# A graph network kernel whose per-graph tail is done for two graphs at a time

## The chip, the cores and the metric

The kernel runs on one core of a Trainium2 chip. The metric is device time in microseconds. TensorE does the matmuls, VectorE and ScalarE the elementwise work out of PSUM, GpSimd elementwise work between SBUF tiles, and SyncE's queue most of the transfers.

## What is computed

There are B = 128 graphs of N = 128 nodes with F = 64 features, the hidden width is H = 192 and the output width 64.

```python
# layer 0, per graph
h   = relu(layernorm(x))
P   = h @ (W1a + W1b) + b1 ;  Q = h @ W1b
hm[j]  = sum over neighbours k of relu(P[j] - Q[k])     # mask = adj > 0
x   = x + hm @ W2 + deg * b2
# layer 1, per graph
h   = relu(layernorm(x))
x   = x + (adj @ h) @ W3.T
```

Each node has some 12% of the others as neighbours. So the kernel doesn't form all 128 x 128 pairs: it numbers the neighbours of each node, and a one-hot matrix per neighbour number picks the row of Q.

## The kernel before

The mask of a graph is turned into codes (a running count of the neighbours) in a set-up that takes about the first 60 us. Then come 128 steps, one per graph, and 4 more to drain the pipeline (`TAIL`). Each engine has its own hand-written `step(b, u)`; `u` is `b` modulo 12.

**The sums of graph b** go through a ring of three PSUM places of two banks each. Four regular chunks (i = 0 to 3) hold four neighbour numbers each:

- ScalarE copies P into the place (`seed`, L530), which is 768 values per partition.
- TensorE adds the picked rows of -Q with 8 matmuls (`gather`, L378), 4 for each bank.
- VectorE takes relu and adds to the accumulator `acc`, one instruction per bank (`consume`, L763).

A chunk's place can be seeded again only when it has been consumed; ScalarE's seed of chunk 1 of a graph waits for the last `consume` of the graph before. A fifth chunk of three slots holds what is left over for nodes with more neighbours: L406 and L378 fill it, ScalarE's L562 takes its relu into `relu_row`, GpSimd's L864 adds the three slots in two instructions, and `ownerT` sends the sums to their nodes in TensorE's L465.

Between its consumes VectorE writes one-hot matrices for later graphs (L749, one between the two consumes of each chunk), `from_first` (L795, after chunk 0), `owner` (L798, chunk 1), `onehot_row` (L804, three instructions after chunk 2) and the low half of PQ (L680, before chunk 3).

**What follows the sums** is done in the steps after, once per graph:

- Step b+1: TensorE transposes the accumulator (L464, four transposes: two slots, and the 192 columns as 128 and 64 padded to 128) and adds the left-over rows (L465, two matmuls). GpSimd puts deg * b2 onto x (L897, L900).
- Step b+2: ScalarE copies the transposed sums (L556), TensorE multiplies by W2 (L441 and L442, 64 columns wide), VectorE adds to x (L813) and takes statistics (L819).
- Step b+3: VectorE's L790 makes mean and variance, GpSimd's four instructions L873, L874, L880 (the power -0.5) and L883 the scale and shift, ScalarE's L583 the normed h2, TensorE the product with the adjacency (L470).
- Step b+4: L556 copies that too, TensorE multiplies by W3 (L445), VectorE adds to x (L816). SyncE's queue stores every four graphs.

GpSimd's order in a step is: L864 twice, the four instructions of the norm, `start_sums` (L851), the low half of P (L890), the bias (L897, L900), and the halves of h1 (L906, L908). ScalarE's order in a step is: seed of chunk 0, copies L550 and L556, seed of chunk 1, L562, copies L567 and L570, seeds of chunks 2 and 3, PQ and P (L575, L576), then L583, which waits for GpSimd's L883, and L591.

Of the kernel before, what the change touches and what calls it, by code (L numbers as in the profile page):

```python
# [53 lines left out]
def gnn_kernel(nc, x, adjT, W1a, W1b, b1, W2, b2, W3T, CONSTS, out):  # L54
# [15 lines left out]
    with ExitStack() as ctx:  # L70
# [13 lines left out]
        w_parts = sb("w_parts", [N, 2, 3 * H], F16)    # L84

        w2a = sb("w2a", [N, O])
        w2b = sb("w2b", [N, O])
        w3t = sb("w3t", [N, O])
# [53 lines left out]
        ownerT = sb("ownerT", [N, 2, N])  # L142
        code_row = sb("code_row", [N, N], F16)
        start = sb("start", [N, PER_BANK, H])
        acc_space = sb("acc", [N, 2, ROW + N - H2])
        acc = acc_space[:, :, 0:ROW].rearrange("p g (s h) -> p g s h", h=H)
        relu_row = sb("relu_row", [N, ROW_SLOTS, H])

        sums_T = sb("sums_T", [N, 3, N])
        hmT, aggT = sums_T[:, 0:2, :], sums_T[:, 2, :]  # L150
        bias = sb("bias", [N, F])
        stats2 = sb("stats2", [N, 6])
        mv = sb("mv", [N, 2, 2])
        ve2 = sb("ve2", [N, 1])
        neg2 = sb("neg2", [N, 2])
        rstd2 = sb("rstd2", [N, 2])
        shift2 = sb("shift2", [N, 2])
        h2 = sb("h2", [N, 2, F])
# [11 lines left out]
        pq_ps, out1_ps, out2_ps = prep[:, 0:2 * H], prep[:, 2 * H:2 * H + O], prep[:, 2 * H + O:2 * H + 2 * O]  # L170
        sums_T_ps = post[:, 0:3 * N].rearrange("p (k n) -> p k n", k=3)
        h1T_ps = post[:, 3 * N:4 * N]
# [58 lines left out]
        sums_T_ready = sem("sums_T_ready")  # L231
# [13 lines left out]
        HEAD, TAIL = 3, 4  # L245
# [42 lines left out]
        def mixed_at(b, u, t):  # L288

            return (u - 3) % BODY, (b - 3) // BODY if isinstance(b, int) else t - 1 if u < 3 else t  # L290
# [21 lines left out]
        def _(sp):  # L312
# [15 lines left out]
            for b in range(3, B + TAIL):  # L328
                if BODY <= b - 3 + BODY < B:
                    sp.wait_ge(transposed, b + 3)  # L330
                    adj(b - 3 + BODY)
                done = b - TAIL + 1
                if done > 0 and done % STORE == 0:
                    sp.wait_ge(y_ready, done)
                    sp.dma_start(out[:, done - STORE:done, :], x_all[:, done - STORE:done, :]).then_inc(stored, 16)
            sp.wait_ge(stored, 16 * B // STORE)

        @block.tensor
        def _(pe):
# [42 lines left out]
            def step(b, u, looped=False, t=None):  # L382
                main = exists(b)
                parts = PQ[:, u % 2]
                for i in range(CHUNKS):
# [25 lines left out]
                    if i == 0 and main:  # L411
# [3 lines left out]
                        if exists(b - 2):  # L415
                            pe.wait_ge(sums_T_ready, b - 1)
                        else:
                            pe.wait_ge(h1T_ready, b + 2)
# [537 lines left out]
```

## Time and profile before

| | |
|---|---|
| time, median of 3 runs | 905.98 us (905.89 to 906.07) |
| time of the profiled execution | 904.65 us |
| its span, first to last instruction | 902.6 us |
| busy share of the span | TensorE 96%, VectorE 96%, ScalarE 86%, GpSimd 77% |
| mean granted TensorE clock | 0.983 of full speed |

The span is what the trace covers, and the execution's time has 2 us around it. Busy spans of neighbouring instructions of one engine overlap in the records, so an engine shown as almost always busy may still have waited; the starts have to be compared.

### The profile page before, as it was taken

To read this page: it belongs to the slowest core of one execution; us is meant where nothing else is said; L and a number is where in the kernel's file an instruction comes from. 1 tells how busy PE (TensorE), PEld (TensorE's weight loads), DVE (VectorE), ACT (ScalarE), POOL (GpSimd) and SP (SyncE) were. 2 spreads that over 40 slices of the span, in tenths; PEclk is the share of its full clock that TensorE was granted. 3 is DMA by queue.
4 is the path that set the end of the run, shared out by engine and by line. 5 is a ranking of instruction groups with operands and counts; after the bars stand their busy time and mean duration, and the time that the engine had idled before them with its cause. 6 is when DMAs were issued, how large, how long until landed. Compare 5 with 4: busy or idle time off the path is not lost.

```text
span 902.6 us, 27715 instructions
## 1 busy us (share of the span) xinstructions
PE 862.0 (96%) x8626; PEld 771.7 (86%) x8627; DVE 866.4 (96%) x3032; ACT 775.9 (86%) x1728; POOL 698.8 (77%) x1548
## 2 busy tenths in 40 slices
PE   3879999999999999999999999999999999999996
PEld 1448999989998989999999999998999899989995
DVE  6989999999999999999999999999999999999993
ACT  4858989898989898989889898988898889898983
POOL 0857787888888888888887878787878788888874
PEclk9789999999999999999999999999999999999997
DMA  9700000000000000000000000000000000000000
GB/s 341 279 1 5 20 11 20 16 20 17 19 17 20 11 20 17 20 17 20 15 14 16 20 17 19 17 18 18 12 20 16 20 16 20 16 20 11 7 8 16
DMA packets 26549, 27.58 MB, mean 31 GB/s; under 512 B 3360, under 2 KB 24352, under 8 KB 25376
## 3 DMA queue, kind: packets, MB, share of 16 engines
q1 hardware_dynamic: 25488, 25.37, 8.3%
q8 instruction: 72, 1.18, 0.6%
q14 instruction: 77, 0.63, 0.2%
q10 hardware_dynamic: 912, 0.39, 0.2%
HBM read 21.56 MB, written 4.19 MB: 29 GB/s over the span
## 4 chain that ended last, share of the span: by engine, by line
PE 69%; DVE 19%; issue 5%; ACT 3%; POOL 2%; DMA 1%; SPq 0%; ACTq 0%; POOLq 0%; DVEq 0%
PE ring L378 36%; DVE acc L763 12%; PE ring L406 6%; PE post L465 4%; PE post L464 4%; PE prep L435 4%; PE post L470 4%; PE prep L445 3%; PE prep L442 2%; DVE onehot_space L749 2%; PE prep L441 2%; ACT ring L530 1%; POOL rstd L915 1%; DMA x_all<-x_nbf_dram 1%; DVE onehot_row L804 1%
## 5 line engine op out<-in xcount | busy, mean ns | idle before, releaser
L763 DVE SCALAR_TENSOR_TENSOR acc<-ring,acc 128x384 f32<-128x384 f32 x896 | 489.0, 546 | 1.1 <-PE ring L378 0.2
L530 ACT COPY ring<-P 128x768 f32<-128x768 f32 x512 | 403.3, 811 | 16.3 <-DVE acc L763 6.9
L378 PE MATMUL ring<-PQ,onehot_space 128*128 128x192 f16 x4096 | 404.0, 247 | 7.2 <-ACT ring L530 3.3
L378 PEld LDWEIGHTS ring<-PQ,onehot_space 128*128 128x128 f16 x4096 | 338.2, 100 | 31.7 <-ACT ring L530 19.2
L864 POOL TENSOR_TENSOR relu_row<-relu_row 128x192 f32<-128x192 f32 x256 | 151.8, 593 | 101.1 <-ACT relu_row L562 91.1
L749 DVE TENSOR_SCALAR onehot_space<-mask_all 128x512 f16<-128x512 f16 x512 | 155.2, 305 | 0.0
L583 ACT ACTIVATE h<-x_all,shift,rstd 128x64 f32<-128x64 f32 x128 | 56.3, 440 | 83.6 <-POOL shift L883 83.6
L851 POOL TENSOR_SCALAR start<-P,spare 128x192 f32<-128x192 f32 x128 | 121.1, 946 | 5.9 <-ACT P L576 5.1
L464 PE MATMUL post<-consts,acc 128*128 128x128 f32 x512 | 98.5, 274 | 1.5 <-POOL relu_row L864 1.5
L465 PE MATMUL post<-ownerT,relu_row 128*128 128x128 f32 x512 | 99.0, 275 | 0.0
L406 PE MATMUL ring<-PQ,owner 128*128 128x384 f16 (+1 forms) x512 | 94.1, 306 | 0.0
L880 POOL TENSOR_TENSOR rstd<-ve,half_power 128x1 f32<-128x1 f32 x128 | 89.4, 698 | 0.0
L378 PE MATMUL ring<-PQ,onehot_row 128*128 128x192 f16 x768 | 84.3, 246 | 0.4 <-DVE onehot_row L804 0.4
L562 ACT ACTIVATE relu_row<-ring 128x576 f32<-128x576 f32 x128 | 82.5, 644 | 0.6 <-PE ring L378 0.6
L763 DVE SCALAR_TENSOR_TENSOR acc<-ring,start 128x384 f32<-128x384 f32 x128 | 71.3, 557 | 11.4 <-PE ring L378 1.6
L465 PEld LDWEIGHTS post<-ownerT,relu_row 128*128 128x128 f32 x512 | 77.3, 191 | 0.0
L378 PEld LDWEIGHTS ring<-PQ,onehot_row 128*128 128x128 f16 x768 | 65.2, 98 | 9.2 <-DVE onehot_row L804 1.1
L890 POOL TENSOR_TENSOR PQ<-P,PQ 128x192 f16<-128x192 f32 x128 | 70.5, 551 | 2.7 <-ACT P L576 2.7
L406 PEld LDWEIGHTS ring<-PQ,owner 128*128 128x128 f16 x512 | 50.5, 99 | 18.2 <-issue 0.2
L575 ACT CAST PQ<-prep 128x384 f16<-128x384 f32 x128 | 63.9, 499 | 0.7 <-PE prep L437 0.7
L470 PE MATMUL post<-adj_again,h 128*128 128x128 f32 x256 | 62.0, 324 | 2.1 <-ACT h L583 2.1
L435 PE MATMUL prep<-w_parts,h1T 128*128 128x384 f16 x256 | 62.9, 328 | 0.9 <-ACT h1T L550 0.9
(129 smaller groups left out, 1616.0 us busy)
## 6 DMA issues: line engine op xcount, KB each, us to landing
onehot_space<-adj_kbj_dram SPq DMA_DIRECT2D x8, 1024.0 KB, 17.1
adj_again<-adj_kbj_dram SPq DMA_DIRECT2D x128, 64.0 KB, 1.9
x_all<-x_nbf_dram SPq DMA_DIRECT2D x8, 512.0 KB, 17.8
out_dram<-x_all SPq DMA_DIRECT2D x32, 128.0 KB, 1.7
consts<-consts_dram SPq DMA_DIRECT2D x1, 192.0 KB, 2.6
scratch<-w1a_dram ACTq DMA_DIRECT2D x2, 48.0 KB, 4.3
scratch<-w1b_dram ACTq DMA_DIRECT2D x2, 48.0 KB, 6.7
scratch<-b_dram ACTq DMA_DIRECT2D x1, 96.0 KB, 10.0
```

The source lines that it names most:

```text
L378: last = nc.tensor.matmul(to, hot(s), parts[:, part, H:2 * H], start=False, stop=(part == 1), skip_group_check=True)
L406: nc.tensor.matmul(slots[place(u, i)][:, bank_, 0:n, :], owner[:, u % 2, :], parts[:, part, 0:H].unsqueeze(1).broadcast_to([N, n, H]), sta ...
L435: nc.tensor.matmul(pq_ps, h1T[:, :], w_parts[:, part, 0:2 * H], start=(part == 0), stop=False, skip_group_check=True)
L464: nc.tensor.matmul(sums_T_ps[:, k, :], hm, ident, start=(s == 0), stop=False, is_transpose=True)
L465: last = nc.tensor.matmul(sums_T_ps[:, k, :], hm_row[:, k * N:(k + 1) * N], ownerT[:, (u + 1) % 2, :], start=False, stop=True)
L470: last = nc.tensor.matmul(sums_T_ps[:, 2, :], h2[:, :, :], adj_again[:, at, :], start=True, stop=True)
L530: return nc.scalar.copy(slots[to], src.unsqueeze(1).unsqueeze(1).broadcast_to([N, BANKS, PER_BANK, H]))
L749: return nc.vector.tensor_scalar(onehot[:, hot_of(u), i, s, :, :], code_kj[:, bass.ds(b, QUAD), :], 2.0 * (SLOTS * i + s) + 1.0, None, ALU ...
L763: return nc.vector.scalar_tensor_tensor(sums, slots[to][:, bank_], 0.0, start[:, :, :] if first else sums, ALU.max, ALU.subtract if first ...
L851: nc.gpsimd.tensor_scalar(start[:, 0, :], P[:, u % 2, :], spare[:, b:b + 1], 0.0, ALU.mult, ALU.max).then_inc(start_ready, 1)
L864: last = nc.gpsimd.tensor_tensor(sums, sums, relu_row[:, s, :], ALU.add)
L880: nc.gpsimd.tensor_tensor(rstd2[:, k:k + 1], ve2[:, :], half_power[:, :], ALU.pow).then_inc(rstd2_ready, 1)
```

## The change

Graphs are taken in pairs of an even and an odd one. The diff cut to its core (the set-up of the new tiles, the helper functions that count semaphores and the names of tiles are left out; `pairs`, `transposes` and `mixes` only give the counts to wait for):

```diff
-        HEAD, TAIL = 3, 4
+        HEAD, TAIL = 3, 5
...
 # TensorE, i == 1
+                            order = slice((u + 1) % 2 * N, (u + 1) % 2 * N + H)
...
-                        if exists(b - 2):
-                            nc.tensor.matmul(out1_ps, hmT[:, 0, :], w2a[:, :], start=True, stop=False)
-                            last = nc.tensor.matmul(out1_ps, hmT[:, 1, :], w2b[:, :], start=False, stop=True)
-                        if exists(b - 4):
-                            last = nc.tensor.matmul(out2_ps, aggT[:, :], w3t[:, :], start=True, stop=True)
+                        if u % 2 and exists(b - 3):
+                            nc.tensor.matmul(out_ps, tailT, w2b[:, :, :], start=True, stop=False, skip_group_check=True)
+                            for g in range(2):
+                                last = nc.tensor.matmul(out_ps[:, g, :], hmT[g], w2a[:, :], start=False, stop=True, skip_group_check=True)
+                        if u % 2 == 0 and exists(b - 6):
+                            last = nc.tensor.matmul(out_ps, aggT, w3t[:, :, :], start=True, stop=True)
 # TensorE, i == 3: the head (128 columns) of each graph, the tails (64 + 64) of a pair at once
+                            for s in range(PER_BANK):
+                                nc.tensor.matmul(head_ps, acc_space[:, (u - 1) // 2 % 2, s, heads[(u - 1) % 2]], ident, start=(s == 0), stop=False, is_transpose=True)
+                            last = nc.tensor.matmul(head_ps, row_heads[(u - 1) % 2], ownerT[:, (u - 1) % QUAD, :], start=False, stop=True)
+                        if u % 2 == 0 and exists(b - 2):
+                            for s in range(PER_BANK):
+                                nc.tensor.matmul(tail_ps, acc_space[:, k // 2, s, tails], ident, start=(s == 0), stop=False, is_transpose=True)
+                            for g in range(2):
+                                last = nc.tensor.matmul(tail_ps, row_tails[g], ownerT[:, k + g, :], start=False, stop=(g == 1))
+                        if u % 2 and exists(b - 5):
+                            for g in range(2):
+                                last = nc.tensor.matmul(agg_ps, h2_padded[g], adj_again[:, at + g, :], start=(g == 0), stop=(g == 1))
 # ScalarE
+                    if i == 0 and u % 2 == 0: nc.scalar.copy(sums_T[:, parts, :], sums_T_ps[:, parts, :])       # 256 wide
+                    if i == 0 and u % 2: nc.scalar.copy(sums_T[:, 2:4, :], sums_T_ps[:, 0:3:2, :])              # 256 wide
                     if i == 1 and exists(b - 1):
                         nc.scalar.activation(relu_rows[(u - 1) % 2], row_slots[place(u, -1)], ACT.Relu)
+                    if i == 1 and u % 2 and exists(b - 5):
+                        norm2(b, u, t, 1)
                     if i == 1 and main:
                         nc.scalar.copy(code_row[:, :], code_row_ps)
...
-                    if i == 4 and exists(b - 3):
+                    if i == 4 and u % 2 == 0 and exists(b - 4):
+                        wait_apart(act, norm2_ready, pairs(b, u, t, -4))
+                        norm2(b, u, t, 0)
 # VectorE
+                    if i == 0 and u % 2 == 0 and exists(b - 4):
+                        for g in range(2):
+                            last = nc.vector.bn_aggr(mv[:, (u - 4) // 2 % 2, g, :], stats2[:, g, :])
+                    if i == 3 and u % 2 and exists(b - 3):
+                        nc.vector.tensor_tensor(x_all[:, pair, :], x_all[:, pair, :], out_ps, ALU.add).then_inc(x1_ready, 1)
+                    if i == 4 and u % 2 and exists(b - 3):
+                        wait_apart(dve, x1_ready, pairs(b, u, t, -3))
+                        for g in range(2):
+                            last = nc.vector.bn_stats(stats2[:, g, :], x_all[:, b - 3 + g, :])
+                    if i == 4 and u % 2 == 0 and exists(b - 6):
+                        nc.vector.tensor_tensor(x_all[:, pair, :], x_all[:, pair, :], out_ps, ALU.add).then_inc(y_ready, 1)
 # GpSimd: the same four instructions of the norm, [N, 2] wide, in even steps alone; the bias [N, 2, F] wide, likewise
+                if u % 2 == 0 and exists(b - 4):
+                    nc.gpsimd.tensor_tensor(rstd2[:, k, :], ve2[:, :], half_power[:, :].broadcast_to([N, 2]), ALU.pow)
```

W2's tail and W3 stand twice in a block-diagonal 128 x 128 matrix; for that two more small loads are issued on ScalarE's queue at the start. The first-layer weights get 128 more columns (a copy on VectorE in the set-up), so that odd graphs come out with their last 64 columns first. `acc` has four buffers in place of two, `relu_row` two in place of one and `ownerT` four in place of two. SyncE's queue loads two adjacency matrices in every second step, and stores when a pair is ready.

## Rows read from the trace of the kernel before

**Rows 1.** VectorE's timeline of one step (start us, us, engine line ...; gaps left out).

```profile
511.47 0.54 DVE L763 SCALAR_TENSOR_TENSOR acc<-ring,acc 128x384 f32<-128x384 f32 x1
...
512.44 0.56 DVE L763 SCALAR_TENSOR_TENSOR acc<-ring,start 128x384 f32<-128x384 f32 x1
...
513.68 0.48 DVE L795 TENSOR_SCALAR from_first<-count_h,first_row 128x128 f16<-128x128 f16 x1
514.07 0.54 DVE L763 SCALAR_TENSOR_TENSOR acc<-ring,acc 128x384 f32<-128x384 f32 x1
514.54 0.39 DVE L749 TENSOR_SCALAR onehot_space<-mask_all 128x512 f16<-128x512 f16 x1
514.85 0.55 DVE L763 SCALAR_TENSOR_TENSOR acc<-ring,acc 128x384 f32<-128x384 f32 x1
...
515.57 0.54 DVE L763 SCALAR_TENSOR_TENSOR acc<-ring,acc 128x384 f32<-128x384 f32 x1
...
516.71 0.38 DVE L804 TENSOR_SCALAR onehot_row<-code_row 128x128 f16<-128x128 f16 x3
...
517.94 0.55 DVE L763 SCALAR_TENSOR_TENSOR acc<-ring,acc 128x384 f32<-128x384 f32 x1
```

**Rows 2.** ScalarE's timeline of the same step.

```profile
512.05 0.80 ACT L530 COPY ring<-P 128x768 f32<-128x768 f32 x1
...
513.64 1.56 ACT L530 COPY ring<-P 128x768 f32<-128x768 f32 x2
...
516.45 0.44 ACT L583 ACTIVATE h<-x_all,shift,rstd 128x64 f32<-128x64 f32 x1 [0.63 <-POOL shift L883]
516.80 0.42 ACT L591 ACTIVATE h<-x_all,shift,rstd 128x64 f32<-128x64 f32 x1
```

**Rows 3.** GpSimd's timeline of the same step, and one power from a step before.

```profile
508.85 0.57 POOL L880 TENSOR_TENSOR rstd<-ve,half_power 128x1 f32<-128x1 f32 x1
...
513.51 1.27 POOL L864 TENSOR_TENSOR relu_row<-relu_row 128x192 f32<-128x192 f32 x2 [0.66 <-ACT relu_row L562]
...
515.35 0.73 POOL L880 TENSOR_TENSOR rstd<-ve,half_power 128x1 f32<-128x1 f32 x1
...
516.39 0.95 POOL L851 TENSOR_SCALAR start<-P,spare 128x192 f32<-128x192 f32 x1
517.31 0.55 POOL L890 TENSOR_TENSOR PQ<-P,PQ 128x192 f16<-128x192 f32 x1
```

**Rows 4.** TensorE's timeline: the gather of chunk 0 consumed at 512.44.

```profile
511.81 0.82 PE L378 MATMUL ring<-PQ,onehot_space 128*128 128x192 f16 x8
```

**Rows 5.** VectorE's timeline of a later step, 615.6 to 622.4.

```profile
615.06 0.54 DVE L763 SCALAR_TENSOR_TENSOR acc<-ring,acc 128x384 f32<-128x384 f32 x1
...
616.08 0.56 DVE L763 SCALAR_TENSOR_TENSOR acc<-ring,start 128x384 f32<-128x384 f32 x1
...
617.66 0.55 DVE L763 SCALAR_TENSOR_TENSOR acc<-ring,acc 128x384 f32<-128x384 f32 x1
...
620.29 0.53 DVE L804 TENSOR_SCALAR onehot_row<-code_row 128x128 f16<-128x128 f16 x3
...
621.89 0.55 DVE L763 SCALAR_TENSOR_TENSOR acc<-ring,acc 128x384 f32<-128x384 f32 x1
```

**Rows 6.** GpSimd's timeline of that later step.

```profile
620.26 1.04 POOL L851 TENSOR_SCALAR start<-P,spare 128x192 f32<-128x192 f32 x1
...
621.27 0.55 POOL L890 TENSOR_TENSOR PQ<-P,PQ 128x192 f16<-128x192 f32 x1
```

**Rows 7.** Groups by line and shape (busy us, mean ns of one record | idle before).

```profile
L442 PE MATMUL prep<-w2b,sums_T 128*128 128x64 f32 x256 | 49.7, 276 | 0.0
...
L816 DVE TENSOR_TENSOR x_all<-x_all,prep 128x64 f32<-128x64 f32 x128 | 26.6, 208 | 3.7 <-PE prep L445 3.7
```

**Rows 8.** Timeline of the set-up: a 32-wide power on GpSimd.

```profile
51.48 5.44 POOL L915 TENSOR_TENSOR rstd<-mom,half_power 128x32 f32<-128x32 f32 x1
```

**Rows 9.** The same stretch on VectorE.

```profile
53.77 2.72 DVE L749 TENSOR_SCALAR onehot_space<-mask_all 128x512 f16<-128x512 f16 x13
```

More of the change, by code:

```diff
@@ L286, in hot_of, with agg_at, transposes, mixes @@
             return u // QUAD % HOT_QUADS
-        def mixed_at(b, u, t):
-            return (u - 3) % BODY, (b - 3) // BODY if isinstance(b, int) else t - 1 if u < 3 else t
+        def agg_at(b, u, t):
+            return (u - 5) % BODY, (b - 5) // BODY if isinstance(b, int) else t - 1 if u < 5 else t
+        def transposes(step):
+            return step + 2 if isinstance(step, int) and step > B + 1 else step + 3
+        def mixes(step):
+            return step + 1 if isinstance(step, int) and step > B + 2 else step + 2
+        def pairs(b, u, t, d):
+            return (b + d) // 2 + 1 if isinstance(b, int) else t * (BODY // 2) + (u + d) // 2 + 1
         def load(eng, which, b):
@@ L326, in _ @@
                 adj(b)
[L328 to L332, printed above, removed]
+            for b in range(0, B, 2):
+                done = b - 2
                 if done > 0 and done % STORE == 0:
-                    sp.wait_ge(y_ready, done)
+                    sp.wait_ge(y_ready, done // 2)
                     sp.dma_start(out[:, done - STORE:done, :], x_all[:, done - STORE:done, :]).then_inc(stored, 16)
+                if b + BODY < B:
+                    sp.wait_ge(transposed, transposes(b + 5))
+                    adj(b + BODY)
+                    adj(b + BODY + 1)
+            sp.wait_ge(y_ready, B // 2)
+            sp.dma_start(out[:, B - STORE:B, :], x_all[:, B - STORE:B, :]).then_inc(stored, 16)
             sp.wait_ge(stored, 16 * B // STORE)
@@ L432, in step @@
+                        last = None
                         if exists(b + 1):
                             pe.wait_ge(h1T_ready, b + 2)
+                            order = slice((u + 1) % 2 * N, (u + 1) % 2 * N + H)
                             for part in range(2):
-                                nc.tensor.matmul(pq_ps, h1T[:, :], w_parts[:, part, 0:2 * H], start=(part == 0), stop=False,
+                                nc.tensor.matmul(pq_ps, h1T[:, :], w_parts[:, part, 0:2, order], start=(part == 0), stop=False,
@@ L466, in step @@
[L466 to L471 removed]
+                            if not main:
+                                pe.wait_ge(even_T_ready, pairs(b, u, t, -2))
```

225 lines of the change are left out of this document (115 added, 110 removed).

## The prediction

> **What bounds the kernel now.** The busy line (in the table ahead) has TensorE and VectorE both at 96%, which doesn't say which of them sets the pace. So I took one step of the timeline and asked of each start what it had waited for. All offsets count from T, the end of a graph's last consume: 511.47 + 0.54 = 512.01 [rows 1]. The next such end is 517.94 + 0.55 = 518.49, 6.48 later; the consumes at 512.44 and at 616.08 lie 16 steps apart [rows 1, 5], 103.64 / 16 = 6.48 us on average. 128 steps make 829 of the 902.6 us.
>
> In this step chunk 0 is consumed at +0.43, chunk 1 at +2.06 and +2.84, chunk 2 at +3.56, and it ends at +6.48 [rows 1]. In the later step T is 615.60; chunk 0 comes at +0.48, but chunk 1 at +2.06 again [rows 5]. So what holds chunk 1 isn't chunk 0. It is GpSimd: L864 starts at +1.50 and its two instructions end at +2.77 [rows 3], the first, by halves, near +2.10. VectorE's L795 lies across that end (513.68, 0.48 long, with the next start 0.39 behind it) and L749 across the end of the second (0.39 long, the next start 0.31 behind); chunk 1's second consume starts 0.07 after GpSimd's end [rows 1, 3]. L749 takes 2.72 / 13 = 0.21 from start to start when it isn't held [rows 9]. I read this as VectorE's f16 instructions and GpSimd's two-input instructions excluding each other. GpSimd's start in turn hangs on T: ScalarE seeds chunk 1 at +0.04 [rows 2], then takes the relu that L864 waits for. This circle (T, seed, relu, L864, chunk 1, 4.42 of VectorE's own work, next T) is 6.48 long and closes by itself. VectorE also waits for chunk 0's gather, 511.81 to 512.44 [rows 4, 1], but has caught up by chunk 1.
>
> **The change, part by part.** *TensorE.* Per pair two transposes, one L442 and one L445 go; the remaining ones of the last two are twice as wide. L442 has 49.7 / 128 = 0.39 us of busy time per graph [rows 7], overlaps included. Four instructions less in a pair, none longer than that, are at most 0.8 us per pair, and half of it if half of the busy time is overlap: I take 0.2 to 0.4 us per graph. It is worth nothing where GpSimd sets chunk 1; without that cover it would be worth the wait for chunk 0, which is the first rival.
>
> *VectorE.* Two of four adds per pair go (L816: 208 ns each [rows 7]) and two become wider; in return `bn_stats` now stands right behind the add on which it waits. Between 0 and 0.2 us per pair, ahead of chunk 0, under the same cover: nothing in even steps.
>
> *GpSimd, even steps.* Chunk 1 is as before. Then the norm's four instructions come for two graphs. The power of 32 values takes 5.44, that of one 0.73 [rows 8, 3], so a second value costs (5.44 - 0.73) / 31 = 0.15; the other three I take as unchanged, being two values wide. So L851 moves from 516.39 (+4.38) to +4.53 and L890 behind it from an end at 517.86 (+5.85) to +6.00 [rows 3]. VectorE's L804 runs at 516.71 (+4.70) [rows 1], now 0.17 behind L851's start in place of 0.32. The later step shows what comes of that: there L851 started at 620.26, +4.66 or 0.28 late, L804 took 0.53 for 0.38, and the last consume started 0.07 after L890's end, at 621.89, +6.29 in place of +5.93 [rows 5, 6, 1]: 0.36 lost for 0.28 of lateness. With L890's end at +6.00 the last consume starts at +6.07, 0.14 late. The bounds are 0 (the second value hides) and 0.36. I take **+0.15 in even steps**, 6.63.
>
> *GpSimd, odd steps.* The norm falls away (L880 to L851 is 1.04 [rows 3]), and the six instructions of norm and bias come once in two steps. GpSimd isn't on the path there; nothing counted.
>
> *VectorE, odd steps.* Ahead of chunk 0 stands one add alone, and no `bn_aggr`, so L795 can start near +1.3, before L864, and isn't held. Chunk 2 could then come at about +2.95, 0.6 early.
>
> *ScalarE, odd steps.* But a second L583 (`norm2(..., 1)`) now stands between the relu of chunk 4 and the two copies and seeds of chunks 2 and 3. It occupies 516.80 - 516.45 = 0.35 [rows 2]. Chunk 2's seed moves from 513.64 (+1.63) to +1.98 and ends 0.80 later, at +2.78 [rows 2]; a gather start to its first consume takes 512.44 - 511.81 = 0.63 [rows 4, 1], with 0.05 for the signal (an estimate from 512.01 to 512.05 for the seed). That is +3.46, against +3.56 before. So **-0.10 in odd steps**: VectorE waits for ScalarE instead. The bounds are -0.6 (the seed isn't late) and +0.1.
>
> *ScalarE, rest.* L556 copies 256 columns in place of 384, 0.1 a step; it idled 0.63 a step [rows 2], and idles on. In even steps L583 comes 0.15 later with GpSimd, and the next seed of chunk 1 with it, but T is 0.15 later as well.
>
> *Queues, set-up, tail.* SyncE's transfers keep their number, in twos; nothing waits for them with 12 buffers. The two new small loads and VectorE's one weight copy lie in the set-up, beside adjacency loads: 0 to 1 us. The drain has one step more, but its transposes no longer stand before the same step's product with the adjacency: -1 to +1. I count 0 for both.
>
> *Sum.* 62 pairs in steady state x (+0.15 - 0.10) = +3.1 us. The profiled execution took 904.65 (span 902.6), so it would come to 907.8; the median of the runs stands 1.3 above it, at 905.98, and goes to **909.1**, which I write 909.0. Own range of this case: both edits uncertain by 0.1 per pair, 902 to 915. A measurement tells some 0.2% (1.8 us) here.
>
> At one place the Trainium skill speaks against the change more strongly than the rows do. Its page "SBUF — State Buffer", section "Who interferes with whom", says that VectorE and GpSimd share one pair of ports as an exclusive lock, held for the whole instruction, so that the second to come blocks fully. The first half is what L864 shows. The second half disagrees with rows 8 and 9: thirteen L749 ran 0.21 apart while the 5.44 us power was in flight. By that rule a longer L880 would also hold chunk 2's L749; it is the third rival.
>
> **The rivals.** *1. TensorE's relief counts* (0.20). If VectorE's wait for chunk 0 is what really sets the step, and L864 only follows, each step loses it: chunk 0 came 0.43 after T, and VectorE's own work in between is two adds and one statistics (208 ns each at most [rows 7], overlapping), so 0.11 to 0.15 goes. 128 x 0.11 to 0.15 = 14 to 19 us: 887 to 892, written 890. For it speaks TensorE's 96%; against it chunk 1 at +2.06 whether chunk 0 was at +0.43 or +0.48 [rows 1, 5].
>
> *2. The second power hides* (0.22). L880 took 0.57 in one step and 0.73 in the next [rows 3], and the spread is as large as a second value's price. If the short form becomes the rule, L851 isn't late, even steps stay at 6.48 or gain a little, and the pair is 0.10 shorter: 62 x -0.10 = -6, so 900. Against it: 0.57 may just be the form that VectorE didn't disturb, and the order of the two engines at that point doesn't change.
>
> *3. The lateness feeds itself* (0.20). Place: L880 to L890 in even steps. If the longer L880 (+3.34 to +4.22) runs into L749 of chunk 2, at 3.56 + 0.47 = +4.03, each delays the other, by 0.06 on VectorE (4.22 + 0.07 against 4.03 + 0.20) and more on GpSimd. It decides from the point where L851 is 0.28 late, as at 620.26; then an even step costs 0.36 [rows 5, 6]. 62 x (0.36 - 0.10) = +16: 922 at the worst, 918 with half of the excess. The case with the lock held for the whole instruction ends here too.
>
> **How the numbers follow.** Forecast 0.38, rival 1 0.20, rival 2 0.22, rival 3 0.20. Faster by over 0.2% (below 904.2): rival 1 whole, 0.20, most of rival 2, 0.16 (if small gains fall short it is within), and of the forecast's own range its lowest tenth, 0.02: 0.38. Within 0.2%: the rest of rival 2, 0.06, and 0.12 of the forecast: 0.18. Slower: 0.24 of the forecast and rival 3: 0.44. The range leaves out the better half of rival 1 and the worst tail of rival 3: 891 to 918.
>
> **What would show it.** Even and odd steps of different lengths, near 6.63 and 6.38. In even steps chunk 1 at +2.06, L880 near 0.88, L851 near +4.53, a longer L804 group, and the last consume 0.07 after L890. In odd steps L795 not held, chunk 1 near +1.5 and an idle VectorE ahead of chunk 2, released by TensorE behind ScalarE's L530. TensorE with more idle time and no gain from it. Wrong would be: chunk 1 of even steps ahead of L864's end (rival 1), L851 at +4.4 (rival 2), or an odd step whose chunk 2 isn't held.

## The result and the profile after

The changed kernel took 913.1 us (911.7 to 914.0, 4 runs), against 906.03 before; the ratio is 1.0077, with a 95% interval of 1.0057 to 1.0097. So it is slower by 0.8%. (Before: three runs from 905.89 to 906.07 and a fourth of 2185 us, which moves the median by 0.05 and is not in the ratio.)

The page of the changed kernel: its span, busy times, and two groups (busy us, mean ns of one | idle before, releaser).

```profile
span 909.7 us, 26109 instructions
...
PE 842.6 (93%) x8242; PEld 718.0 (79%) x8243; DVE 851.5 (94%) x2908; ACT 761.9 (84%) x1728; POOL 614.1 (68%) x1164
...
L808 DVE SCALAR_TENSOR_TENSOR acc<-ring,acc 128x384 f32<-128x384 f32 x896 | 490.3, 547 | 27.7 <-PE ring L400 26.8
...
L904 POOL TENSOR_SCALAR start<-P,spare 128x192 f32<-128x192 f32 x128 | 120.0, 938 | 96.5 <-ACT P L618 95.7
```

Every engine does less work, TensorE by 19.4 us, VectorE by 14.9, GpSimd by some 85, and the kernel is longer. (L808 is the consume, before L763; L904 the start of the sums, before L851; L943 the low half of P, which completes PQ and is called the halves of PQ below, before L890; L918 the row sums, before L864; L960 and L962 the split of h into halves, before L906 and L908; L794 the one-hot, before L749; L851 is now VectorE's one-hot rows, before L804; L933 the power, before L880.)

To split the 7.1 us of span, one line per kernel is enough: a step's first consume, with its first and last start. Before:

```profile
L763 DVE SCALAR_TENSOR_TENSOR acc<-ring,start x128: 532/558/560, 58.9 to 881.7; 128x384 f32<-128x384 f32 x128
```

and after:

```profile
L808 DVE SCALAR_TENSOR_TENSOR acc<-ring,start x128: 539/558/559, 60.3 to 889.2; 128x384 f32<-128x384 f32 x128
```

The set-up is 1.4 longer, the 127 steps between are 828.9 in place of 822.8, so 6.1 longer (6.527 each in place of 6.479), and what follows is 0.4 shorter. Now one even and one odd step, with offsets from T, the end of a graph's last consume. VectorE's timeline of the changed kernel:

```profile
516.32 0.55 DVE L808 SCALAR_TENSOR_TENSOR acc<-ring,acc 128x384 f32<-128x384 f32 x1
...
518.93 0.54 DVE L808 SCALAR_TENSOR_TENSOR acc<-ring,acc 128x384 f32<-128x384 f32 x1
...
520.89 0.28 DVE L794 TENSOR_SCALAR onehot_space<-mask_all 128x512 f16<-128x512 f16 x1
521.09 0.54 DVE L808 SCALAR_TENSOR_TENSOR acc<-ring,acc 128x384 f32<-128x384 f32 x1
521.56 0.54 DVE L851 TENSOR_SCALAR onehot_row<-code_row 128x128 f16<-128x128 f16 x3
...
522.75 0.39 DVE L794 TENSOR_SCALAR onehot_space<-mask_all 128x512 f16<-128x512 f16 x1
523.06 0.54 DVE L808 SCALAR_TENSOR_TENSOR acc<-ring,acc 128x384 f32<-128x384 f32 x1
...
525.12 0.55 DVE L808 SCALAR_TENSOR_TENSOR acc<-ring,acc 128x384 f32<-128x384 f32 x1
...
527.04 0.56 DVE L808 SCALAR_TENSOR_TENSOR acc<-ring,acc 128x384 f32<-128x384 f32 x1 [0.44 <-PE ring L400]
...
529.41 0.55 DVE L808 SCALAR_TENSOR_TENSOR acc<-ring,acc 128x384 f32<-128x384 f32 x1
```

and GpSimd's in the even one of the two:

```profile
520.01 0.23 POOL L929 TENSOR_SCALAR neg<-mv 128x2 f32<-128x2 f32 x1
520.21 1.00 POOL L933 TENSOR_TENSOR rstd<-ve,half_power 128x2 f32<-128x2 f32 x1
521.35 0.20 POOL L936 TENSOR_TENSOR shift<-neg,rstd 128x2 f32<-128x2 f32 x1
521.53 0.94 POOL L904 TENSOR_SCALAR start<-P,spare 128x192 f32<-128x192 f32 x1
522.44 0.55 POOL L943 TENSOR_TENSOR PQ<-P,PQ 128x192 f16<-128x192 f32 x1
```

T is 516.32 + 0.55 = 516.87, 523.60 and 529.96. The even step is 6.73 long, the odd one 6.36. In the even step chunk 1 comes at 518.93, +2.06 as before. The power lasts 1.00, the start of the sums comes at +4.66 in place of +4.38 [rows 3], the one-hot rows take 0.54 for 0.38 [rows 1], the last L794 0.39 for 0.28 (before: the line below), and the last consume starts 0.07 behind L943's end, 522.99. The two lengthened instructions are 0.16 + 0.11 = 0.27, and 6.73 - 0.27 is 6.46.

```profile
517.74 0.28 DVE L749 TENSOR_SCALAR onehot_space<-mask_all 128x512 f16<-128x512 f16 x1
```

In the odd step chunk 1 comes at +1.52, then VectorE waits 0.44 for the gather of chunk 2, which comes at +3.44. Such pairs are 0.13 longer than two steps of before (2 x 6.479); 64 of them would be 8.3, and 6.1 were measured, so not all pairs are of this form. In the middle of the run (steps 10 to 115, 53 pairs) the pairs are 6.1 longer together, 0.115 each: four of the even steps there take 6.47 to 6.61, and two of the steps before take 6.73 and 6.84. The steps in which the pipeline fills and drains differ little.

### The profile page after: what moved, and what is told of

The parts are those of the page before. It is cut to its first block, busy times and chain, and to the rows that moved or that the text cites. A ratio compares the mean times of both kernels' runs of the same rounds, so it can differ in the third digit from the quotient of the medians.

```text
span 909.7 us, 26109 instructions
## 1 busy us (share of the span) xinstructions
PE 842.6 (93%) x8242; PEld 718.0 (79%) x8243; DVE 851.5 (94%) x2908; ACT 761.9 (84%) x1728; POOL 614.1 (68%) x1164
## 4 chain that ended last, share of the span: by engine, by line
DVE 52%; PE 19%; issue 16%; ACT 9%; DMA 1%; POOL 1%; SPq 0%; DVEq 0%; ACTq 0%; POOLq 0%
DVE acc L808 31%; PE ring L400 10%; DVE onehot_space L794 7%; ACT ring L561 5%; DVE onehot_row L851 4%; DVE PQ L725 3%; PE prep L465 2%; PE prep L457 2%; DVE stats L865 2%; ACT row_space L604 1%; DVE x_all L861 1%; DMA x_all<-x_nbf_dram 1%; PE prep L463 1%; DVE mv L836 1%; DVE owner L845 1%
## 5 line engine op out<-in xcount | busy, mean ns | idle before, releaser
L808 DVE SCALAR_TENSOR_TENSOR acc<-ring,acc 128x384 f32<-128x384 f32 x896 | 490.3, 547 | 27.7 <-PE ring L400 26.8
L400 PE MATMUL ring<-PQ,onehot_space 128*128 128x192 f16 x4096 | 412.5, 247 | 32.5 <-ACT ring L561 19.9
L400 PEld LDWEIGHTS ring<-PQ,onehot_space 128*128 128x128 f16 x4096 | 319.6, 98 | 97.4 <-ACT ring L561 50.0
L918 POOL TENSOR_TENSOR row_space<-row_space 128x192 f32<-128x192 f32 x256 | 151.8, 593 | 125.7 <-ACT row_space L604 115.6
L904 POOL TENSOR_SCALAR start<-P,spare 128x192 f32<-128x192 f32 x128 | 120.0, 938 | 96.5 <-ACT P L618 95.7
L794 DVE TENSOR_SCALAR onehot_space<-mask_all 128x512 f16<-128x512 f16 x512 | 155.1, 305 | 0.0
L566 ACT ACTIVATE h<-x_all,shift,rstd 128x64 f32<-128x64 f32 x128 | 55.5, 434 | 60.0 <-POOL shift L936 60.0
L604 ACT ACTIVATE row_space<-ring 128x576 f32<-128x576 f32 x128 | 82.4, 644 | 0.7 <-PE ring L400 0.7
L808 DVE SCALAR_TENSOR_TENSOR acc<-ring,start 128x384 f32<-128x384 f32 x128 | 71.3, 557 | 5.2 <-PE ring L400 2.6
L943 POOL TENSOR_TENSOR PQ<-P,PQ 128x192 f16<-128x192 f32 x128 | 70.0, 547 | 2.7 <-ACT P L618 2.7
L933 POOL TENSOR_TENSOR rstd<-ve,half_power 128x2 f32<-128x2 f32 x64 | 62.1, 971 | 0.0
L851 DVE TENSOR_SCALAR onehot_row<-code_row 128x128 f16<-128x128 f16 x384 | 59.2, 208 | 0.0
L631 ACT ACTIVATE h<-x_all,shift,rstd 128x64 f32<-128x64 f32 x128 | 57.5, 449 | 0.1
L960 POOL TENSOR_SCALAR h_parts<-h 128x64 f16<-128x64 f32 x128 | 54.4, 425 | 2.9 <-ACT h L631 2.9
L487 PE MATMUL post<-consts,acc 128*128 128x128 f32 x256 | 49.7, 276 | 1.8 <-issue 1.8
```

What stands on the lines that cost most here:

```text
L400: last = nc.tensor.matmul(to, hot(s), parts[:, part, H:2 * H], start=False, stop=(part == 1), skip_group_check=True)
L604: nc.scalar.activation(relu_rows[(u - 1) % 2], row_slots[place(u, -1)], ACT.Relu).then_inc(relu_row_ready, 1)
L794: return nc.vector.tensor_scalar(onehot[:, hot_of(u), i, s, :, :], code_kj[:, bass.ds(b, QUAD), :], 2.0 * (SLOTS * i + s) + 1.0, None, ALU ...
L808: return nc.vector.scalar_tensor_tensor(sums, slots[to][:, bank_], 0.0, start[:, :, :] if first else sums, ALU.max, ALU.subtract if first ...
L851: last = nc.vector.tensor_scalar(onehot_row[:, s, :], code_row[:, :], 2.0 * (COVERED + s) + 1.0, None, ALU.is_equal)
L904: nc.gpsimd.tensor_scalar(start[:, 0, :], P[:, u % 2, :], spare[:, b:b + 1], 0.0, ALU.mult, ALU.max).then_inc(start_ready, 1)
```

## The experiments

Twelve kernels ran. "Start" below is the start of the sums on GpSimd; offsets are again from T. The diffs are cut to the lines that matter; waits and semaphore increments that only follow from the new order, and `.then_inc(...)` at the ends of lines, are left out.

**e1, the power alone.** GpSimd's power is taken for the even graph of a pair only; the odd graph's is left out (its `rstd` is 1). All else is the changed kernel.

```diff
-nc.gpsimd.tensor_tensor(rstd2[:, k, :], ve2[:, :], half_power[:, :].broadcast_to([N, 2]), ALU.pow)
+nc.gpsimd.tensor_tensor(rstd2[:, k, 0:1], ve2[:, 0:1], half_power[:, :], ALU.pow)
```

> The changed kernel with GpSimd's power for the even graph of a pair alone (the scale of odd graphs stays at 1.0: the power of the second graph is left out). Everything else stays paired. Theory (GpSimd's lateness in even steps): the power falls from 0.97 to 0.70 us, L851 starts 0.27 earlier, even steps fall from 6.73 to 6.47, odd steps stay at 6.36. 62 pairs x 0.26 = 16 us: 897 us, ratio to the kernel before 0.990. Rival (the lost time lies in the paired TensorE and VectorE work or in the set-up, GpSimd has room at 68% busy): 911 to 913, ratio 1.006 to 1.008.

Measured: 902.4 us, ratio to the kernel before 0.9973 (0.9962 to 0.9984). The power's group in e1 and in the changed kernel (ns min/median/max):

```profile
L934 POOL TENSOR_TENSOR rstd<-ve,half_power x64: 557/722/724, 88.6 to 893.1; 128x1 f32<-128x1 f32 x64
```

```profile
L933 POOL TENSOR_TENSOR rstd<-ve,half_power x64: 715/1001/1006, 88.7 to 902.2; 128x2 f32<-128x2 f32 x64
```

The whole loss hangs on this one instruction, which is 0.28 us shorter 64 times: the even steps fall from 6.73 to 6.47. The odd steps came out longer than expected, 6.47 for 6.36, so that less was gained than 16 us: with T 0.26 earlier, GpSimd's split of h (L963 here) now lies across VectorE's first L795 of the next step, which lasts 0.44, and `from_first` is caught by the row sums:

```profile
518.63 0.56 DVE L809 SCALAR_TENSOR_TENSOR acc<-ring,start 128x384 f32<-128x384 f32 x1
519.11 0.44 DVE L795 TENSOR_SCALAR onehot_space<-mask_all 128x512 f16<-128x512 f16 x1
519.47 0.55 DVE L809 SCALAR_TENSOR_TENSOR acc<-ring,acc 128x384 f32<-128x384 f32 x1
519.93 0.54 DVE L843 TENSOR_SCALAR from_first<-count_h,first_row 128x128 f16<-128x128 f16 x1
520.39 0.54 DVE L809 SCALAR_TENSOR_TENSOR acc<-ring,acc 128x384 f32<-128x384 f32 x1
```

With T at 518.34 chunk 1 is at +2.05 again, in an odd step, whose early chunk 1 is lost. GpSimd's start comes at +4.23 there, and the one-hot rows, 0.45 behind it, are not lengthened (GpSimd first, then VectorE):

```profile
522.57 1.03 POOL L905 TENSOR_SCALAR start<-P,spare 128x192 f32<-128x192 f32 x1 [1.48 <-ACT P L618]
```

```profile
523.02 0.38 DVE L852 TENSOR_SCALAR onehot_row<-code_row 128x128 f16<-128x128 f16 x3
```

**e2, the odd graph's norm on ScalarE** moved from ahead of chunk 2's seed to behind chunk 3's.

```diff
-                    if i == 1 and u % 2 and exists(b - 5):
+                    if i == 3 and u % 2 and exists(b - 5):
                         norm2(b, u, t, 1)
```

> The changed kernel with ScalarE's norm of the odd graph moved from behind the relu of chunk 4 to behind the seed of chunk 3, so that the seeds of chunks 2 and 3 come 0.35 us earlier in odd steps. Theory (ScalarE's queue holds chunk 2 in odd steps): chunk 2's seed goes from +1.95 to +1.62, its first consume from +3.44 to about +3.1 at the latest, and odd steps from 6.36 to about 6.0, unless VectorE's own work is what is left; even steps stay at 6.73. 62 x 0.3 = 19 us: 894, range 890 to 900. Rival (VectorE or TensorE is the bound in odd steps, and the seed only looks late): 911 to 914.

Measured: 909.0 us, ratio 1.0042 (1.0026 to 1.0059). Chunk 2 came 0.23 earlier, and 0.16 of it went to the next collision. VectorE's rows in an odd step of e2 (T = 522.24; GpSimd's start is at 526.47, +4.23):

```profile
525.45 0.56 DVE L808 SCALAR_TENSOR_TENSOR acc<-ring,acc 128x384 f32<-128x384 f32 x1 [0.22 <-PE ring L400]
...
526.59 0.55 DVE L851 TENSOR_SCALAR onehot_row<-code_row 128x128 f16<-128x128 f16 x3
```

The rows take 0.55 there, and 0.39 in the changed kernel, where GpSimd's start is at +4.23 too but the rows come 0.23 later.

**e3, the norm split:** the odd graph's power and shift go into the odd step, behind the row sums, and its ScalarE norm to the step's end.

```diff
+                if u % 2 and exists(b - 5):
+                    nc.gpsimd.tensor_tensor(rstd2[:, k, 1:2], ve2[:, 1:2], half_power[:, :], ALU.pow)
+                    nc.gpsimd.tensor_tensor(shift2[:, k, 1:2], neg2[:, k, 1:2], rstd2[:, k, 1:2], ALU.mult)
```

> The changed kernel with GpSimd's power and shift split: the even graph's in the even step, the odd graph's in the odd step behind L864, and ScalarE's norm of the odd graph at the end of the odd step, as in the even step. TensorE, VectorE, bias, variance and mean stay paired. Theory: both holds go at once: even steps 6.47, odd steps near 6.0; pair 12.5 against 13.1: 62 x 0.6 = 37 us: 876, range 870 to 885, and below the kernel before, since the wait on TensorE and two instructions of VectorE are really saved. Rival (the holds are the old ones and the paired work isn't worth anything): 905 to 907, as before the change.

Measured: 931.8 us, ratio 1.0284 (1.0261 to 1.0308), the largest miss so far. VectorE and GpSimd in an odd step of e3 (T = 519.27):

```profile
524.14 0.89 DVE L854 TENSOR_SCALAR onehot_row<-code_row 128x128 f16<-128x128 f16 x3
```

```profile
523.19 0.93 POOL L907 TENSOR_SCALAR start<-P,spare 128x192 f32<-128x192 f32 x1 [0.23 <-ACT P L618]
524.09 0.55 POOL L953 TENSOR_TENSOR PQ<-P,PQ 128x192 f16<-128x192 f32 x1
```

GpSimd isn't late here, it is early: its start came at +3.92, and the halves of PQ lie right across the one-hot rows, 0.89 for 0.38. So "GpSimd late" can't be the whole rule.

**e4, TensorE's relief alone**, in the kernel before: the transposes and the product of the last 64 columns of the accumulator are left out.

```diff
-                            nc.tensor.matmul(out1_ps, hmT[:, 0, :], w2a[:, :], start=True, stop=False)
-                            last = nc.tensor.matmul(out1_ps, hmT[:, 1, :], w2b[:, :], start=False, stop=True)
+                            last = nc.tensor.matmul(out1_ps, hmT[:, 0, :], w2a[:, :], start=True, stop=True)
...
-                                for s in range(PER_BANK):
+                                for s in range(PER_BANK if k == 0 else 0):
```

> The kernel before the change, with TensorE's two transposes of the last 64 columns and the multiplication by W2's tail left out (the last 64 columns of the sums of regular chunks don't reach the output): some 0.44 us less TensorE work per graph, more than the 0.33 that the change saves. Theory (chunk 1 is held by GpSimd's L864): steps stay at 6.47 to 6.48, 904 to 906, ratio 0.998 to 1.0. Rival 1 of the prediction (VectorE's wait for chunk 0's gather sets the step): 887 to 892, ratio 0.98.

Measured: 903.6 us, ratio 0.9985 (0.9976 to 0.9995). The line of its first consumes:

```profile
L762 DVE SCALAR_TENSOR_TENSOR acc<-ring,start x128: 535/558/560, 59.7 to 881.1; 128x384 f32<-128x384 f32 x128
```

A step is 6.468 for 6.479: TensorE's spare time is worth 0.01 a step, not the 0.11 to 0.15 of the first rival. How much was taken off is less than expected, though: TensorE's busy time falls from 862.0 to 846.6 us, 0.12 a graph and not 0.44, while the change took off 0.15 a graph. So e4 tests nearly the relief of the change, not more than it.

**e5, the wide power in the kernel before**, every step, its second value unused.

```diff
-nc.gpsimd.tensor_tensor(rstd2[:, k:k + 1], ve2[:, :], half_power[:, :], ALU.pow)
+nc.gpsimd.tensor_tensor(rstd2[:, k, :], ve2[:, :], half_power[:, :].broadcast_to([N, 2]), ALU.pow)
```

> The kernel before the change, with GpSimd's power (L880) computed on two columns in every step, the second a copy that nobody reads: the suspected cost of the change alone, twice as often. Theory (a GpSimd that is 0.27 us late at L851 and L890 holds VectorE's L804 and the one-hot matrix of chunk 3): every step goes from 6.47 to 6.73, 128 x 0.26 = 33 us: 938, ratio 1.036. Rival (GpSimd is busy 77% of the span and the wait is taken up, only TensorE's L470 gets later and VectorE catches up behind L864): 906 to 909.

Measured: 933.4 us, ratio 1.0314 (1.0282 to 1.0347). The power's group is 1.00 as in the changed kernel, and the first consume runs from 58.8 to 908.6, 6.69 a step:

```profile
L880 POOL TENSOR_TENSOR rstd<-ve,half_power x128: 724/1002/1005, 81.3 to 921.8; 128x2 f32<-128x2 f32 x128
```

So the second value alone costs about 0.21 in each step that has it, in a kernel that has nothing else of the change. (The `ve` ahead of the power is two values wide as well there, and lasts 0.22 at either width.)

**e6, power first.** In the changed kernel the power stands right behind `ve`, the variance with epsilon; the start of the sums and PQ follow, negation and shift come behind them, and ScalarE's norms move to the odd step.

```diff
-                    nc.gpsimd.tensor_scalar(neg2[:, k, :], mv[:, k, :, 0], -1.0, None, ALU.mult)
...
-                    nc.gpsimd.tensor_tensor(shift2[:, k, :], neg2[:, k, :], rstd2[:, k, :], ALU.mult)
...
                         start_sums(b + 1, u + 1)
...
+                    nc.gpsimd.tensor_scalar(neg2[:, k, :], mv[:, k, :, 0], -1.0, None, ALU.mult)
...
+                    nc.gpsimd.tensor_tensor(shift2[:, k, :], neg2[:, k, :], rstd2[:, k, :], ALU.mult)
```

> The changed kernel with GpSimd's order turned: the pair's power right behind the epsilon, then L851 and L890, and the negated mean and the shift behind them; ScalarE norms both graphs in the odd step (one behind the relu of chunk 4, one at the end). All work is there and paired, the 0.97 us power too. Theory: L851 starts at +4.2 to +4.4 in even steps, 0.3 earlier than in the changed kernel, and they fall to 6.47; odd steps stay at 6.36 if the one-hot matrix of chunk 0 gets the port before GpSimd's L962 (else 6.47, as most of them in the run with the narrow power). 897 to 903, ratio 0.992 to 0.998. Rival (the two-wide power costs its 0.27 us wherever it stands): 911 to 914.

Measured: 929.9 us, ratio 1.0278 (1.0261 to 1.0295), far off. VectorE and GpSimd in an even step of e6 (T = 513.50):

```profile
517.51 0.45 DVE L791 TENSOR_SCALAR onehot_space<-mask_all 128x512 f16<-128x512 f16 x1
...
518.35 0.76 DVE L848 TENSOR_SCALAR onehot_row<-code_row 128x128 f16<-128x128 f16 x3
```

```profile
516.64 0.72 POOL L929 TENSOR_TENSOR rstd<-ve,half_power 128x2 f32<-128x2 f32 x1
517.40 0.94 POOL L901 TENSOR_SCALAR start<-P,spare 128x192 f32<-128x192 f32 x1
518.31 0.55 POOL L936 TENSOR_TENSOR PQ<-P,PQ 128x192 f16<-128x192 f32 x1
```

Two things are new. The two-value power takes 0.72, not 1.00, when it is over before the one-hot of chunk 2 begins. And GpSimd is early again: start at +3.90, both one-hot groups longer, the even step 7.02.

**e7, e3 with one more wait:** in odd steps GpSimd's start waits until the one-hot rows are written.

```diff
+                        if u % 2:
+                            pool.wait_ge(onehot_row_ready, b + 1)
                         start_sums(b + 1, u + 1)
```

> The kernel with the split norm (it took 931.8), with one more wait: in odd steps GpSimd starts L851 only when VectorE has written onehot_row. Theory (there GpSimd was too early, not too busy: L851 at +3.91 and L890 at +4.81 lay on VectorE's one-hot matrix of chunk 2 and on L804, and odd steps took 7.11): the wait takes that away, odd steps fall to 6.47 or below (6.1 to 6.2 where chunk 0 isn't held): 903, range 888 to 906. Rival (four more instructions per pair on GpSimd, or a later start of the sums, are what costs): 925 or above.

Measured: 897.9 us, ratio 0.9921 (0.9904 to 0.9937). An added wait took 34 us out. (The profiled execution took 901.8, the others 897.6 to 898.0, so the trace, with steps of 6.46 and 6.47, doesn't show why e7 ends 7 us under the kernel before.) Start at +5.27 in an odd step of e7 (T = 518.05), behind the rows (0.38):

```profile
522.74 0.38 DVE L854 TENSOR_SCALAR onehot_row<-code_row 128x128 f16<-128x128 f16 x3
```

```profile
523.32 0.93 POOL L907 TENSOR_SCALAR start<-P,spare 128x192 f32<-128x192 f32 x1 [1.59 <-DVE onehot_row L854]
```

**e8, e6 with bias and norms in the odd step,** where GpSimd has its gap.

```diff
+                if u % 2 and exists(b - 3):
+                    nc.gpsimd.tensor_tensor(bias[:, :, :], ...)
+                    nc.gpsimd.tensor_tensor(x_all[:, of, :], x_all[:, of, :], bias[:, :, :], ALU.add)
                     start_sums(b + 1, u + 1)
...
-                if u % 2 == 0 and exists(b - 2):
-                    nc.gpsimd.tensor_tensor(bias[:, :, :], ...)
-                    nc.gpsimd.tensor_tensor(x_all[:, of, :], x_all[:, of, :], bias[:, :, :], ALU.add)
```

> The turned order of GpSimd (power first), and besides the pair's bias (two instructions) moved from the end of even steps into the gap of odd steps between L864 and L851, and both of ScalarE's norms at the end of odd steps, so that chunk 2's seed is early. All work is there. Theory: even steps 6.47; in odd steps chunk 0's one-hot matrix is free, chunk 2 comes at +3.21 and L851 near +3.85, L890 between L804 and the one-hot matrix of chunk 3, so 3.21 + 2.91 = 6.12. Pair 12.6: 62 x -0.36 = -22 against the kernel before: 883, range 878 to 892, ratio 0.975. Rival (the holds only move on to another pair of instructions): 897 or above.

Measured: 920.1 us, ratio 1.0166 (1.0149 to 1.0183). An even step of e8 went from 522.09 to 529.11 and the odd one behind it to 535.29 (ends of last consumes). So the odd half held, 6.18; the even one was 7.02 by e6's collision, which this expectation, made together with e6's, shared.

**e9, one instruction moved:** in the changed kernel the negation goes behind the power, so the power starts 0.2 earlier.

```diff
-                    nc.gpsimd.tensor_scalar(neg2[:, k, :], mv[:, k, :, 0], -1.0, None, ALU.mult)
                     nc.gpsimd.tensor_tensor(rstd2[:, k, :], ve2[:, :], half_power[:, :].broadcast_to([N, 2]), ALU.pow)
+                    nc.gpsimd.tensor_scalar(neg2[:, k, :], mv[:, k, :, 0], -1.0, None, ALU.mult)
```

> The changed kernel with one GpSimd instruction moved: in even steps the negation of the mean stands behind the power instead of ahead of it, so that the power starts 0.2 us earlier. Theory (a power that VectorE's one-hot of chunk 2 doesn't lie across costs 0.72 us for two values, as in the earlier run with the power first; 0.97 is the one-hot in its way, from 4.02 to 4.30 behind T): the power 0.73 in place of 0.97, the start of the sums at +4.38 in place of +4.65, even steps 6.47 in place of 6.73. Odd steps lose some of their gain, as with the narrow power, because the split of h now ends 0.25 later against the new T and lies across VectorE's first one-hot: 6.45. In all 902 us, range 897 to 905. Rival (the second value itself costs 0.25): nothing moves, since the instructions are the same and their sum too: 911 to 913.

Measured: 912.7 us, ratio 1.0085 (1.0071 to 1.0098), as the rival had it, but not for its reason. GpSimd and VectorE in an even step of e9 (T = 516.77):

```profile
519.91 0.73 POOL L932 TENSOR_TENSOR rstd<-ve,half_power 128x2 f32<-128x2 f32 x1
520.72 0.38 POOL L933 TENSOR_SCALAR neg<-mv 128x2 f32<-128x2 f32 x1
521.19 0.20 POOL L936 TENSOR_TENSOR shift<-neg,rstd 128x2 f32<-128x2 f32 x1
521.37 0.99 POOL L904 TENSOR_SCALAR start<-P,spare 128x192 f32<-128x192 f32 x1
```

```profile
520.79 0.28 DVE L794 TENSOR_SCALAR onehot_space<-mask_all 128x512 f16<-128x512 f16 x1
```

The power shrank to 0.73, as the theory had it. But now the negation lies across VectorE's L794 (+4.02 to +4.30), takes 0.38 for 0.23 and ends 0.03 after it, at +4.33. In the changed kernel it was the power that ended at +4.34. VectorE's one-hot holds whichever of these two GpSimd instructions meets it, and lets GpSimd's chain go on at about +4.3 in both.

**e10, e8 with negation and shift ahead of the start again.**

> The kernel with bias and both norms' activations in the odd step (920 us), with one change: negation and shift stand ahead of the start of the sums again, right behind the early power. Theory (that run was slow because in even steps the start of the sums at +3.90 and the halves of PQ at +4.81 came too early and lay across the one-hot of chunk 2 and the one-hot rows): start at +4.38, the halves at +5.28 behind the one-hot rows, even steps 6.47 in place of 7.02; odd steps stay at 6.18. 62 x (0.55) less: 886 us, range 880 to 894; it would beat both kernels and every run so far. Rival (something else in that order is slow, a wait of ScalarE's for the norms or of the drain): above 905.

Measured: 904.4 us, ratio 0.9993 (0.9984 to 1.0002), far from the 886 expected. Odd steps 6.18 as expected; the negation met L794 as in e9, the start came at +4.66, and the even steps were 6.74 (row sums of e10 at 526.75 and 533.49).

**e11, e10 with the start behind the one-hot rows in even steps,** the wait of e7 with `u % 2 == 0`.

> The same kernel as e10, but in even steps the start of the sums waits for VectorE's one-hot rows as well, so it comes at about +5.28, 0.6 later than in the changed kernel (4.65), and 0.9 later than in e10. Theory (what counts is whose instruction lies across whose, not how late GpSimd is): even steps 6.47, 0.26 shorter than in the changed kernel though GpSimd is later; the odd steps lose their gain, because the split of h then ends beyond +1.1 of them: 6.2 to 6.47. In all 885 to 902. Rival (each 0.1 that the start of the sums is later costs about as much, as +0.27 cost +0.26 in the changed kernel): even steps 7.2 or more, above 925.

Measured: 939.0 us, ratio 1.0377 (1.0362 to 1.0391), the slowest of all. VectorE in an even step of e11 (T = 517.98; GpSimd's start at 523.25, +5.27), and the rows of the odd step after it:

```profile
522.67 0.38 DVE L847 TENSOR_SCALAR onehot_row<-code_row 128x128 f16<-128x128 f16 x3
...
523.90 0.54 DVE L804 SCALAR_TENSOR_TENSOR acc<-ring,acc 128x384 f32<-128x384 f32 x1
...
529.35 0.84 DVE L847 TENSOR_SCALAR onehot_row<-code_row 128x128 f16<-128x128 f16 x3
```

The even step is 524.44 - 517.98 = 6.46, as the theory had it: GpSimd 0.6 later than in the changed kernel and the step 0.27 shorter, which refutes the rival. The total was missed because of the odd steps. The split of h ends later in them, chunk 1 falls back to +2.06, the rows come 0.55 later than in e10, and GpSimd's early start (528.35, +3.91) puts the halves of PQ across them: 0.84, and a step of 7.11.

**e12, the start placed:** e8 with one wait, the start of the sums behind VectorE's one-hot of chunk 2 in even steps.

```diff
+                    if s == 2 and exists(b):
+                        last.then_inc(third_hot, 1)
...
+                        if u % 2 == 0 and exists(b - u % QUAD + QUAD):
+                            pool.wait_ge(third_hot, b + 1)
                         start_sums(b + 1, u + 1)
```

> The kernel with bias and both norms' activations in the odd step (920 us), with one wait added: in even steps the start of the sums waits for VectorE's one-hot of chunk 2, so it comes at about +4.36 where it came at +3.90. Negation and shift stay behind it. Theory (from the runs so far an even step is 6.47 with the start of the sums at 4.37, 6.73 at 4.60 to 4.66, 7.02 at 3.90, and 6.47 again at 5.27): start +4.36, halves of PQ about +5.27, one-hot rows from +4.69 at 0.10 apart, even steps 6.47; odd steps stay 6.18, since the split of h ends near +0.5 of them and their first one-hot comes at +0.59. 61 pairs x 0.55 less than 920: 886 us, range 880 to 895. Rival (what is left over in that order, negation, shift and split behind the halves of PQ, now lies across the next step's first one-hots and its early chunk 1 is lost): odd steps 6.47, about 903. Second rival (the window is narrower than thought and the rows are still held): even steps 6.7, about 903 too; the two differ in the parity that is long.

Measured: 895.6 us, ratio 0.9891 (0.9873 to 0.9909): the fastest of all, with the whole of the work done, 1.1% under the kernel before and 1.8% under the changed one (0.9891 / 1.0077). It is slower than the 886 expected and just outside the range of 880 to 895: the start came at +4.50, not +4.36, since the signal took 0.2, and even steps are 6.57, not 6.47. In an even step of e12 (T = 521.22):

```profile
525.72 0.94 POOL L903 TENSOR_SCALAR start<-P,spare 128x192 f32<-128x192 f32 x1 [0.63 <-DVE onehot_space L791]
```

```profile
525.90 0.49 DVE L850 TENSOR_SCALAR onehot_row<-code_row 128x128 f16<-128x128 f16 x3
```

Read together, the steps whose chunk 1 comes at +2.06 go by one quantity, the place of GpSimd's start, whatever the kernel and the parity:

| GpSimd's start | one-hot rows (0.38 alone) | step | kernel |
|---|---|---|---|
| +3.90 | 0.76 | 7.02 | e6, even |
| +3.92 | 0.89 | 7.11 | e3, odd |
| +4.23 | 0.38 | 6.47 | e1, odd |
| +4.38 | 0.38 | 6.48 | before |
| +4.50 | 0.49 | 6.57 | e12, even |
| +4.60 | 0.53 | 6.72 | e9, even |
| +4.66 | 0.54 | 6.73 | changed, even |
| +5.27 | 0.38 | 6.46 | e7, odd; e11, even |

Where chunk 1 comes at about +1.5 another timetable holds: in the odd steps of e8 and e10 the start is at +3.91, the rows begin at +4.36 and take 0.53, and the step is 6.18 all the same.

## Why the prediction was right, and where it was off

The direction and the range (891 to 918) held; 909.0 was forecast, 913.1 measured. That the direction held is in part luck: the forecast of +0.05 per pair was the difference of two terms, +0.15 and -0.10, and smaller than the 0.1 by which it was called uncertain.

**The circle through GpSimd's row sums** held: chunk 1 at +2.06 in the even steps, and e4 shows that TensorE's relief gives 0.01 a step in the kernel before. Rival 1 is refuted. The busy shares had said nothing of it. Two things are not shown. No run moved the row sums themselves; that they hold chunk 1 is read from the rows, and from the odd steps, where `from_first` begins 0.14 ahead of them (524.96 against 525.10) and chunk 1 comes at +1.52. And no run tells whether the odd steps, whose chunk 0 comes at +0.22, need TensorE's relief. That relief was 19.4 / 128 = 0.15 us of busy time per graph, less than the 0.2 to 0.4 of the prediction.

**Even steps, the mis-sized term.** The prediction said: "so a second value costs (5.44 - 0.73) / 31 = 0.15", and took +0.15 for the step, 6.63. Measured: the power +0.28 (0.722 to 1.001, medians of e1 and of the changed kernel), L904 at +4.66 for +4.53, the step 6.73. The consequence it drew, a longer L804 group and the last consume 0.07 behind L890's end, is what the rows show, and e1 and e5 show that the power is its cause. The size failed because the power was priced as if alone. A two-value power that meets no one-hot is 0.725 (medians of e6 and e12), a one-value power in the quiet place of e7's odd step 0.617: the second value is then worth some 0.11, near the 0.15 (an estimate, since VectorE's `owner` lies inside the power of e6 and e12 and not inside e7's). The rest is the one-hot of chunk 2, which the longer power meets.

```profile
L931 POOL TENSOR_TENSOR rstd<-ve,half_power x64: 713/725/727, 88.1 to 885.3; 128x2 f32<-128x2 f32 x64
```

```profile
L944 POOL TENSOR_TENSOR rstd<-ve,half_power x64: 548/617/627, 94.0 to 893.0; 128x1 f32<-128x1 f32 x64
```

(The first line is e12's, the second e7's.)

**Rival 3** had named that place: "If the longer L880 (+3.34 to +4.22) runs into L749 of chunk 2". It does, but only GpSimd pays: L794 stays 0.28 while the power goes to 1.00. The lateness then grows from 0.15 to 0.28 and stops there; the step cost 0.25, not its 0.36. (In the step from which the 0.36 was taken the start itself lasted 1.04 [rows 6], here 0.94.) So the measured time lies between forecast and rival 3. The rival's 918 "with half of the excess" doesn't follow from its numbers: half of the way from 909.0 to 922 is 915.5. Rival 2 (the second value hides) is refuted by e5.

The Trainium skill, "SBUF — State Buffer", section "Who interferes with whom", gives an exclusive lock on the pair of ports that VectorE and GpSimd share, held for the whole of an instruction. For VectorE's one-hots as holders the trace agrees in one half: in e9 the negation ended 0.03 behind L794. But the page gives the pair to whichever starts first, and the negation had started at 520.72, L794 at 520.79. For GpSimd's start as holder it disagrees: in e12 it runs from 525.72 to 526.66, and the one-hot rows inside of it, from 525.90, end at 526.39, lengthened by only 0.11. The page also says that a VectorE instruction with at most one input in SBUF, outside the modes that use two ports, stays out of it; the trace agrees for the consumes (PSUM and SBUF in), which take 0.54 to 0.56 wherever GpSimd is. No run here shows in which mode the one-hots run.

**Odd steps** came as forecast: 6.36 for 6.38, chunk 1 at +1.52 for "near +1.5", chunk 2 at +3.44 for +3.46, released by TensorE behind ScalarE. But ScalarE's norm was not the only thing that kept the rest of the gain away. I had bounded it at -0.6 without the norm, and e2 gave 0.06: next in line are the gather itself (0.22 of waiting left) and the one-hot rows, which then meet GpSimd's start. e10 shows what is to be had when both are moved, 6.18.

**The sum.** By the trace: steps +6.1 for +3.1, set-up +1.4 for 0, the rest -0.4 for 0; together 7.1 for 3.1. The set-up's share stays open: the first consume came at 58.8 to 59.7 in e4, e5 and the kernel before, and at 59.7 to 60.7 in the kernels made from the changed one, so part of it may be chance, and no experiment was made on it.

**What stays open.** Why a start at +4.38 leaves the rows alone and one at +4.50 doesn't: one-hot rows that begin 0.03 to 0.19 behind the start are lengthened, those 0.31 to 0.37 behind it are not, so there is a hold within its first half, but the rows don't show what GpSimd does then. Nor is this the whole rule: 0.45 behind the start either engine can lose. In most odd steps of e1 the rows take 0.38 and the start 1.03, in four of them, and in e10's odd steps, the rows 0.53 and the start 0.93. Nor was it tried to move the even steps' `bn_aggr`, which stands ahead of `from_first` and may be what keeps chunk 1 of even steps at +2.06.

## What to carry to other kernels

When two engines exclude each other, their order within a step is a timetable: here the same GpSimd instruction cost nothing at +4.23 to +4.38 and at +5.27, and 0.10 to 0.63 us in between or at +3.9. So price a longer or a moved instruction by what it will lie across, on both engines, and not by its length; and when a step loses, try first to place the instruction with a wait, as e7 and e12 did, before taking work away. Work saved on engines off the circle (here 19 us of TensorE, 15 of VectorE, 85 of GpSimd) bought nothing as long as the power and the start stood badly.

## What the runs showed that I had not expected

- A one-hot on VectorE of 0.28 us stretches a GpSimd instruction of two values that meets it: the power 0.73 to 1.00 (e9 against the changed kernel), the negation 0.23 to 0.38 (changed kernel against e9).
- Making GpSimd earlier can cost more than making it later: e3 and e6, with the start at about +3.9 in steps whose chunk 1 is at +2.06, lost 0.5 to 0.6 in each of these; an added wait gave 34 us back (e3 to e7).
- A GpSimd wait for a VectorE signal took 0.2 us here: e12's one-hot ended at 525.51 (525.23 + 0.28 of its L791) and GpSimd went on at 525.72.
